# The constant rows of q_aug and k_aug: laid by SyncE from a scratch copy instead of by GpSimd from the inputs

## What is computed

```
x = x + 0.5 * ffn(layernorm(x))         # ffn: down(silu(gate(x)) * up(x)), hidden width 768, integer weights / 127
x = x + attention(layernorm(x))         # 16 heads of 16 channels
x = x + 0.5 * ffn(layernorm(x))

# attention, per head:
bias   = -slope[h] * abs(pos_q - pos_k)
scores = (q @ k.T) * 16 ** -0.5 + bias
out    = softmax(scores) @ v            # then @ Wo.T + bo
```

## Time and profile before

| what | before |
|---|---|
| median of 3 runs | 937.38 us (936.65 to 939.65) |
| span of the profiled execution, first to last instruction | 934.4 us |
| busy: PE, DVE, ACT, POOL | 90%, 70%, 56%, 46% |
| first ffn, attention, second ffn (roughly, by the turns of TensorE) | to 204 us, to 780 us, to the end |

### The profile page before, as it was taken

One profiled execution on the slowest core, in us unless ns is written; L12 is line 12 of the kernel. 1 busy time (PEld: TensorE's weight loads), 2 busy tenths in 40 slices (PEclk: granted clock), 3 DMA queues, 4 the chain that ended last, 5 costly groups with the idle time before them and its releaser, 6 DMA issues.

```text
span 934.4 us, 15958 instructions
## 1 busy us (share of the span) xinstructions
PE 842.8 (90%) x4672; PEld 579.8 (62%) x4672; DVE 653.1 (70%) x1359; ACT 526.3 (56%) x745; POOL 430.1 (46%) x490
## 2 busy tenths in 40 slices
PE   3809999896999999999999999999999998999988
PEld 2708888783555556556555555565565445888887
DVE  5708878667767767767767777767768736677775
ACT  5304344350566866876866867757767676334443
POOL 0424433351454644644645645635646355434443
PEclk9968999995899999999999999999999999999999
DMA  9130000028357166166076085085184000000001
GB/s 348 51 57 19 0 0 0 2 48 225 90 136 187 43 162 160 43 164 178 20 180 179 3 216 145 18 223 121 33 228 100 2 2 1 26 32 35 22 22 47
DMA packets 40854, 83.38 MB, mean 89 GB/s; under 512 B 7568, under 2 KB 8592, under 8 KB 40624
## 3 DMA queue, kind: packets, MB, share of 16 engines
q1 hardware_dynamic: 35824, 80.16, 32.2%
q0 software_dynamic: 4480, 2.18, 1.3%
q10 hardware_dynamic: 512, 0.53, 0.2%
HBM read 44.56 MB, written 37.75 MB: 88 GB/s over the span
## 4 chain that ended last, share of the span: by engine, by line
PE 72%; DVE 11%; issue 7%; DMA 4%; ACT 3%; POOL 1%; ACTq 0%; DVEq 0%; SPq 0%; POOLq 0%
PE ps L962 66%; DVE row_max L875 4%; DMA q_aug<-max_row 3%; DVE xn L724 2%; PE ps L1013 2%; PE ps L974 2%; PE ps L1018 1%; DVE hid L775 1%; PE ps L1023 1%; ACT gated L583 1%; DMA k_aug<-parts_scratch 1%; ACT stage L627 1%; DVE w_max L832 1%; DMA parts_scratch<-parts 1%; PE ps L999 1%
## 5 line engine op out<-in xcount | busy, mean ns | idle before, releaser
L875 DVE TENSOR_REDUCE row_max<-ps 128x1 f32<-128x512 f32 x512 | 341.3, 687 | 128.7 <-PE ps L962 127.3
L671 ACT ACTIVATE probs<-ps 128x1024 f32<-128x1024 f32 x256 | 252.4, 1022 | 100.2 <-PE ps L962 89.9
L548 POOL TENSOR_TENSOR probs<-probs,diag 128x256 f32<-128x256 f32 x256 | 187.1, 733 | 232.8 <-ACT probs L671 232.6
L962 PE MATMUL ps<-k_aug,q_aug 96*128 96x512 f32 x512 | 222.0, 459 | 13.7 <-DVE row_max L875 6.8
L962 PE MATMUL ps<-xnt,wgu_r 128*128 128x512 f32 x768 | 185.2, 400 | 31.3 <-DVE hid L775 24.5
L481 POOL TENSOR_TENSOR hid_r<-hid,hid_r 128x512 fp32r<-128x512 f32 x96 | 124.1, 1294 | 175.5 <-ACT hid_r L577 175.2
L962 PEld LDWEIGHTS ps<-k_aug,q_aug 96*128 96x128 f32 x512 | 95.9, 195 | 146.2 <-DVE row_max L875 125.2
L962 PEld LDWEIGHTS ps<-xnt,wgu_r 128*128 128x128 f32 x768 | 146.4, 193 | 64.8 <-DVE hid L775 26.4
L962 PE MATMUL ps<-q_aug,k_aug 98*128 98x512 f32 x512 | 159.6, 405 | 8.1 <-DMA q_aug<-max_row 8.1
L962 PE MATMUL ps<-probs,v_aug 128*32 128x512 f32 x1024 | 137.9, 611 | 0.8 <-POOL probs L548 0.8
L583 ACT ACTIVATE gated<-ps 128x512 f32<-128x512 f32 x96 | 57.4, 598 | 119.3 <-PE ps L962 119.3
(11 more groups left out here) (64 smaller groups left out, 691.8 us busy)
## 6 DMA issues: line engine op xcount, KB each, us to landing
parts_scratch<-parts SPq DMA_DIRECT2D x128, 256.0 KB, 5.7
q_aug<-parts_scratch SPq DMA_DIRECT2D x32, 512.0 KB, 4.8
k_aug<-parts_scratch SPq DMA_DIRECT2D x32, 512.0 KB, 6.5
x_sb<-x_in SPq DMA_DIRECT2D x8, 512.0 KB, 12.7
x_out<-x_sb SPq DMA_DIRECT2D x8, 512.0 KB, 2.6
wgu_i<-w_gate_up SPq DMA_DIRECT2D x2, 768.0 KB, 6.0
k_aug<-k_bias POOLq DMA_DIRECT2D x2, 544.0 KB, 11.0
w_att<-w_att SPq DMA_DIRECT2D x1, 1024.0 KB, 11.2
```

The costliest lines, as they stand in the source:

```text
L548: nc.gpsimd.tensor_tensor(tile, tile, diag[:, n * QH + 2 * pair:n * QH + 2 * pair + 2, :], ALU.mult).then_inc(fixed, 1)
L671: nc.scalar.activation(probs[:, kt % 2, 2 * pair:2 * pair + 2, :], ps[:, at:at + 2, :], ACT.Exp).then_inc(exp_done, 1)
L875: nc.vector.reduce_max(row_max[:, quad % 2, u % TT, u // TT:u // TT + 1], max_bank(b, tile)[0], mybir.AxisListType.X).then_inc(s1_used, 1)
L962: return nc.tensor.matmul(out, lhs, rhs, start=start, stop=stop, **k)
```

## The change

SyncE copies the two constant inputs to two new tensors in device memory early on, between the last load of x and the load of `bo`. Later it waits for the same two semaphores as `lay_rows` did, and for the copies, and issues two DMAs from the copies to the rows of `q_aug` and `k_aug`, all 16 heads in each. The destination is addressed as float32 (`bitcast(F32)`), where GpSimd's DMAs addressed it as float32r and the source as float32. GpSimd keeps only the memset and its wait for `w_ready`. TensorE waits for 2 DMAs instead of 4.

```diff
+    d_qrows = nc.dram_tensor("q_rows_scratch", (4 * NSEG, H, L), F32).ap()
+    d_krows = nc.dram_tensor("k_rows_scratch", (ROWS - ROW_BIAS, L), F32).ap()
...
+            sp.dma_start(d_qrows, d_qb).then_inc(rows_in, 16)
+            sp.dma_start(d_krows, d_kb).then_inc(rows_in, 16)
             sp.dma_start(bo[:], d_bo.to_broadcast([P, C])).then_inc(att_in, 16)
             sp.dma_start(diag[:], d_diag).then_inc(att_in, 16)
+
+            sp.wait_ge(watt_ready, 1)
+            sp.wait_ge(w_ready, KC + 1)
+            sp.wait_ge(rows_in, 16 * 2)
+            sp.dma_start(q_aug[ROW_BIAS:ROW_MAX, :, :].bitcast(F32), d_qrows).then_inc(aug_in, 16)
+            sp.dma_start(k_aug[ROW_BIAS:ROWS, :, :].bitcast(F32),
+                         d_krows.rearrange("r (o t) -> r o t", o=1).to_broadcast([ROWS - ROW_BIAS, H, L])
+                         ).then_inc(aug_in, 16)
...
-            def lay_rows():
+            def lay_ones():
 
                 pool.wait_ge(w_ready, KC + 1)
-                pool.wait_ge(watt_ready, 1)
-                for h in range(0, H, H // 2):
-                    pool.dma_start(q_aug[ROW_BIAS:ROW_MAX, h:h + H // 2, :], d_qb[:, h:h + H // 2, :]).then_inc(aug_in, 16)
-                    pool.dma_start(k_aug[ROW_BIAS:ROWS, h:h + H // 2, :],
-                                   d_kb.rearrange("r (o t) -> r o t", o=1).to_broadcast([ROWS - ROW_BIAS, H // 2, L])
-                                   ).then_inc(aug_in, 16)
                 nc.gpsimd.memset(v_aug[:], 1.0).then_inc(ones_set, 1)
                 pool.wait_ge(ones_set, 1)
...
-            pe.wait_ge(aug_in, 16 * 4)
+            pe.wait_ge(aug_in, 16 * 2)
```

More of the change, by code:

```diff
@@ L328, in build_program @@
             sem(n) for n in ("dn_in", "eye_in", "watt_in", "att_in", "aug_in", "stored"))
+        rows_in = sem("rows_in")
         w_ready, w_seen, w_reduced, beyond_ready = (sem(n) for n in ("w_ready", "w_seen", "w_reduced", "beyond_ready"))
@@ L485, in split_hidden @@
                 if w == 0 and first(b):
-                    lay_rows()
+                    lay_ones()
             turns(pool, lambda b: split_hidden(0, b))
```

## The result

| what | before | after |
|---|---|---|
| median of 4 runs | 938.51 us (936.65 to 940.66) | 915.08 us (911.37 to 917.76) |
| ratio | | 0.9744, 95% interval 0.9713 to 0.9775 |
| span of the profiled execution | 934.4 us | 915.9 us (its own time: 917.76 us) |
| turn 1 of the first ffn | 39.32 to 83.67 us | 39.02 to 59.66 us |
| first scores of attention | 215.87 us | 191.00 us |

The change takes 23.4 us off the median, 2.6%. The page of the changed kernel shows where: the third slice of TensorE, which was 0, is 9, the clock's is 9 instead of 6, and the software queue q0 is gone from the DMA queues (slices are now 22.9 us).

What follows compares the result with a forecast made beforehand. TensorE, busy 90% of the span, was taken as the bound, with a hole in turn 1 of the first ffn. 22.09 + 1.75 = 23.84 us off the 937.38 us median gave 913.5 us, range 909.5 to 919 us.

Steps and rivals of the forecast that it cites:

- The hole, 22.09 us: Turn 1, first ffn: TensorE idles from 48.37 to 70.46 us behind GpSimd's late split; all 22.09 us go.
- the sum: Turn 1 of the first ffn: 22.09 us of hole plus 1.75 us of clock, 23.84 us gained.
- That VectorE keeps up: Turn 1 of the first ffn: VectorE follows despite statistics of two sequences; the 1.75 us gain depends on it.
- The clock, 1.75 us: Rest of turn 1 from tile 4: without the low clock it takes 11.46 instead of 13.21 us, 1.75 us gained.
- The inference from the 51 GB/s and the time of the fourth issue: GpSimd's 18.25 us wait: the fourth DMA issue lacks descriptor room until the slow k_aug transfer has finished.
- The rival in which the profile's "issue" was GpSimd's code: GpSimd's stall is code fetching, not DMAs, and remains after the memset: 11.0 us gained, 926.4 us; chance 3%.
- VectorE's hold on a shared port: Form of the 3% not-the-DMAs rival: VectorE holding the shared port pair blocks GpSimd's descriptor writes during the 22.09 us.
- The copies and the transfers, 0 us: SyncE's four added DMAs: 0 us on the path, rows there between 58 and 86 us, over 100 us of cover.
- a change in the length of this stretch: Sign of error: TensorE's first scores to the end not keeping its length.
- the rival in which part is given back: Attention's clock and late loop code return part of the gain: 9% for 917 to 920 us, 3% for under 910.
- a bound of 0 to 5 us: TensorE's "issue" waits at loop ends, if code arrives late behind large transfers: 0 to 5 us, taken as 0.
- The slower rival: SyncE held or rows landing late, TensorE waiting for aug_in: a loss with rows later than 215.9 us; chance 1%.

Runs made afterwards that it cites:

- weights_early: The changed kernel with VectorE making the low parts of the attention weights before turn 0 instead of after it: 911.76 us, ratio 0.9711.
- again: The changed kernel run once more, nothing altered: 913.37 us, ratio 0.9735.
- ring5120: The kernel before with 5120 instead of 4096 bytes for the descriptors of GpSimd's DMAs: median 1.5 us above the expected 919 us.
- split32: The kernel before with the 34 k_aug rows of each half in two DMAs, 32 and 2 rows: 917.97 us, ratio 0.9788.
- pool_scratch: The changed kernel with GpSimd again laying the rows in four DMAs, from the scratch copies, addressed as float32: 939.81 us, ratio 1.0014.
- late6: The changed kernel with SyncE's two transfers held until after turn 5 of the first ffn, issued at 136.70 us: 913.75 us, ratio 0.9743.
- again2: The changed kernel run another time, unaltered, beside other kernels on the same chip: 914.68 us, ratio 0.9744.
- ring4352: The kernel before with 4352 instead of 4096 bytes for the descriptors of GpSimd's DMAs: one execution, 940.75 us.
- late8: The changed kernel with SyncE's two transfers held until after turn 7 of the first ffn: 941.68 us, ratio 1.0027.

## Why the prediction was right

**The hole, 22.09 us.** Right. Turn 1 shrank from 44.35 to 20.64 us, by 23.71 us, where the sum said 23.84. The chain that replaced it ran nearly as worked out: memset over at 38.3 us (38.7 forecast), first split at 44.80 us (45.1), turn 2 at 59.66 us (59.83).

**That VectorE keeps up.** Not quite. The third `hid` was there at 47.3 us, but the fourth only at 50.3 us, behind the statistics of two sequences, and TensorE idled 0.46 us before tile 5. I had looked at tile 4 alone. In weights_early, where VectorE's two weight instructions don't stand at the head of turn 1, the 48 matmuls run without this gap.

**The clock, 1.75 us.** Right in this stage. From the end of tile 4, at about 48.1 us, to turn 2 TensorE took 11.6 us, where the sum said 11.46. The granted clock was at its higher level in all of turn 1 (0.95 in this execution, 1.00 in again), and the page's clock row has its first 6 only in the ninth slice, 183 to 206 us, where attention starts.

**What causes the stall.** The inference from the 51 GB/s and the time of the fourth issue held. More room alone (ring5120) and more engines alone (split32) each take the wait away, and the addressing does not (pool_scratch). The same wait at 4096 and 4352 bytes and none at 4608 fit that the four DMAs must have room together; the count behind that, 280 descriptors, is an estimate. The rival in which the profile's "issue" was GpSimd's code falls with these; VectorE's hold on a shared port was ruled out by its 0.75 us of work.

**The copies and the transfers, 0 us.** Right; pool_scratch and late6 show it for each. The first scores moved from 215.87 to 191.00 us, a little more than the 23.84 us; in the other executions of the changed kernel they came at 190.26 us (again) and 193.45 us (again2).

**What came back.** From the first scores to the end the profiled execution of after took 724.9 us, before 718.5 us, 6.4 us more. The prediction had named a change in the length of this stretch as a sign that it was wrong, and this looks like the rival in which part is given back. The profile of after names two places. At the entry of the second ffn TensorE waited 2.46 us for "issue", and a few microseconds at the clock's lower level followed:

```profile
754.38 2.48 PE L969 MATMUL ps<-xnt,wgu_r 128*128 128x512 f32 x8 [2.46 <-issue]
757.37 4.83 PE L969 MATMUL ps<-xnt,wgu_r 128*128 128x512 f32 x16
```

In the profile of before there was no such wait. But it isn't the change's: ring4352, which is the kernel before in all but 256 bytes, has it with 2.48 us, and pool_scratch, which keeps the hole too, with 2.34 us:

```profile
773.80 2.79 PE L968 MATMUL ps<-xnt,wgu_r 128*128 128x512 f32 x8 [2.34 <-issue]
```

Of all the profiles only that of before lacks it and that of split32 nearly does (0.61 us). The prediction had a bound of 0 to 5 us for such a wait and put it at nothing; its sum starts from the median, and not from the one profiled execution that had none. The other place is attention. Most of its turns in this execution took 68.6 us where the clock column shows 0.95, and 68.1 us in before, where it shows 1.00; one turn of each:

```profile
369.93:438.05 68.12, 66.55 (x380) 40.27 (x376) 50.05 (x87) 48.29 (x66) 37.38 (x50) 1.00 0.50 124
...
344.55:413.13 68.58, 67.20 (x382) 40.30 (x376) 50.11 (x87) 48.38 (x65) 37.49 (x50) 0.95 0.50 123
```

The 0.95 too is a thing of this one execution; in again the same kernel ran at 1.00. That it made the turns longer is not shown: turn 1 of the first ffn took 20.64 us at 0.95 and 20.65 us at 1.00 in again, and again's turns of attention, from the third on, took 68.1 to 68.9 us. From the first scores to the second ffn, after took 563.4 us, again 559.9 us and before 559.1 us; the second ffn took 161.5, 161.8 and 159.4 us, the shortest where the wait at its entry was missing. In ring4352, with the hole in place, first scores to the end took 723.1 us, nearer to after than to before. So the 6.4 us are, as far as these profiles tell, scatter between executions and not a price of the change. The medians, not the two profiled spans, say what the change is worth, and by them it is 23.4 us here, 24.6 us in again and 24.1 us in again2. The prediction said 23.84 us. I had taken the 3.0 us between the profiled span and the median as a fixed distance. The profiled execution of after shows only 1.9 us between its span and its own time; the rest was scatter between executions. That the median of the changed kernel came within 1.6 us of the forecast owes something to luck, since its own executions lie 6.4 us apart.

**The slower rival.** It didn't come about, but it is real: late8 is it, made by hand. My price for it, a microsecond for each microsecond that the rows are late, was too low. The rows would have been there at about 205 us, 14 us too late; the first scores came 30 us late, for the most part because SyncE was held for 18.8 us in the issues behind them.

## What to carry to other kernels

A wait of "issue" in front of a DMA issue is to be read together with the GB/s column: where the wait ends when an earlier transfer ends, and that transfer creeps at an even low rate, look at the number of partitions, and split 34 rows into 32 and 2 before anything is moved to another engine. Where a transfer must be slow, issue it from the queue that has nothing to do for a long time behind it, and compute how long that is: here a transfer of 22 us was free with 130 us of room and still with 40 us (late6), and cost 28 us of the median when its queue was needed at once (late8 against late6), a few of them the added wait's own. A hole in which all engines stand still behind one could be priced well here: hole, plus the low clock behind it, minus what is next in line.

## What the runs showed of the hardware

- A DMA over 34 partitions moved at 51 GB/s at a share of 0.13 to 0.17 of 16 engines, issued by GpSimd or by SyncE; with the rows split into 32 and 2 the queues reached 208 GB/s, the rows of `q_aug` beside them.
- GpSimd waited 18.25 and 18.12 us with descriptor areas of 4096 and 4352 bytes, and not at all with 4608 and 5120: a step, not a slope. The wait ended some 2 us after the earlier transfer, not when part of it was done.
- SyncE, too, can be held by a transfer that runs on few engines: 21.88 us for four issues that take 2.47 us when the rows are split, 19.3 us of it in the first issue.
- TensorE waited for "issue" at the entry of the second ffn for 2.3 to 2.9 us in nearly all profiles, for 0.61 us in split32 and not at all in before. In the three profiles of the changed kernel it was 2.46, 2.86 and 2.54 us, so it doesn't explain their 911 to 918 us.
